# Eight-batch attention and spline FFN kernel: TensorE's loop turned elsewhere, the first batch's gathers in a row, and two kinds of products merged

## The reference

```python
h = depthwise_causal_conv(x, cond[:, None, :]) + cond_b          # 8 taps
q, k, v = split(h @ qkv_w.T + qkv_b)                             # 16 heads of 32
s = q @ k.T / sqrt(32) + slope[h] * (key - query)                # ALiBi, causal
x = x + softmax(where(causal, s, -1e9)) @ v @ out_w.T + out_b
Q, K, V = W @ x[b]          # c = the 256 rows, t = the 512 channels; 16 heads of 16
a = (Q.T @ K / 4 + b0) * m + (1 - m) * -1e30                     # m = cond[b], over keys
y = softmax(a) @ V
gate_w, up_w, down_w = catmull_rom(control_points)               # 2048 x 512 each
x = x + (silu(y @ gate_w.T) * (y @ up_w.T)) @ down_w.T
```

## Time and profile before

| | us |
|---|---|
| median of 3 runs | 1441.94 |
| lowest, highest | 1441.18, 1443.64 |
| the profiled execution, its own time | 1434.63 |
| its span, first to last instruction | 1432.8 |
| busy: TensorE, its weight loads | 1244.2, 725.6 |
| busy: VectorE, ScalarE, GpSimd | 755.2, 521.8, 359.6 |

### The profile page before, as it was taken

One profiled execution on the slowest core, in us unless ns is written; L12 is line 12 of the kernel. 1 busy time (PEld: TensorE's weight loads), 2 busy tenths in 40 slices (PEclk: granted clock), 3 DMA queues, 4 the chain that ended last, 5 costly groups with the idle time before them and its releaser, 6 DMA issues.

```text
span 1432.8 us, 23277 instructions
## 1 busy us (share of the span) xinstructions
PE 1244.2 (87%) x8680; PEld 725.6 (51%) x8680; DVE 755.2 (53%) x1173; ACT 521.8 (36%) x698; POOL 359.6 (25%) x203
## 2 busy tenths in 40 slices
PE   4485379899889999899999999899998998999988
PEld 3152135555455555556455555555455564656445
DVE  5354463547534673457724575346733577346732
ACT  1221145323532245223542245223552235423562
POOL 3079810055000830038000650009200380000000
PEclk9697579999989999999998999799998999999999
DMA  9857722366043731256042650337222560437124
GB/s 330 236 197 204 220 83 59 98 159 185 6 105 120 175 106 46 61 164 215 22 104 82 145 173 15 91 124 193 84 54 53 165 214 22 104 124 189 62 104 162
DMA packets 80495, 181.12 MB, mean 126 GB/s; under 512 B 14404, under 2 KB 54292, under 8 KB 70708
## 3 DMA queue, kind: packets, MB, share of 16 engines
q1 hardware_dynamic: 78352, 175.21, 41.9%
q0 software_dynamic: 1280, 4.20, 1.1%
q10 hardware_dynamic: 768, 0.26, 0.1%
HBM read 106.41 MB, written 21.14 MB: 89 GB/s over the span
## 4 chain that ended last, share of the span: by engine, by line
PE 66%; DVE 12%; issue 5%; POOL 5%; SPq 5%; DMA 4%; ACT 2%; DVEq 0%; ACTq 0%; POOLq 0%
PE psum L1054 8%; PE psum L848 8%; PE psum L1004 7%; PE psum L890 6%; DVE max L760 5%; PE psum L891 4%; PE psum L892 4%; PE psum L854 4%; SPq L374 3%; PE psum L879 3%; PE psum L868 3%; PE psum L916 3%; PE psum L1040 3%; PE psum L973 2%; PE psum L938 2%
## 5 line engine op out<-in xcount | busy, mean ns | idle before, releaser
L760 DVE TENSOR_REDUCE max<-psum 128x1 f32<-128x512 f32 x512 | 329.0, 685 | 113.0 <-PE psum L1004 110.9
L619 ACT ACTIVATE probs<-psum 128x1024 f32<-128x1024 f32 x256 | 248.8, 1022 | 119.0 <-PE psum L1040 118.3
L1004 PE MATMUL psum<-k,q 52*128 52x512 f32 x512 | 169.9, 514 | 75.4 <-DVE max L760 49.8
L505 POOL TENSOR_TENSOR h<-h_in,tap 128x1024 f32<-128x1024 f32 x7 | 13.3, 1900 | 701.3 <-DVE low L674 701.3
L1004 PEld LDWEIGHTS psum<-k,q 52*128 52x128 f32 x512 | 65.2, 191 | 197.8 <-DVE max L760 136.3
L580 ACT ACTIVATE probs<-psum 128x1024 f32<-128x1024 f32 x64 | 62.1, 1022 | 211.8 <-PE psum L959 211.8
L1054 PE MATMUL psum<-probs,v 128*32 128x256 f32 x2048 | 138.7, 389 | 0.4 <-ACT probs L619 0.3
L848 PE MATMUL psum<-h,qkv_w 128*128 128x256 f32 x512 | 119.8, 389 | 18.0 <-DVE h L653 18.0
L515 POOL TENSOR_TENSOR h<-h,products 128x1024 f32<-128x1024 f32 x49 | 128.0, 2611 | 3.8
L848 PEld LDWEIGHTS psum<-h,qkv_w 128*128 128x128 f32 x512 | 96.4, 193 | 39.1 <-issue 26.6
L890 PE MATMUL psum<-stack 128*128 128x512 f32 x256 | 113.7, 444 | 1.3 <-DVE stack L693 1.2
(11 more groups left out here) (106 smaller groups left out, 1722.9 us busy)
## 6 DMA issues: line engine op xcount, KB each, us to landing
stack<-wd_sorted SPq DMA_DIRECT2D x64, 1024.0 KB, 5.8
stack<-high SPq DMA_DIRECT2D x128, 128.0 KB, 2.4
stack<-low SPq DMA_DIRECT2D x64, 128.0 KB, 2.4
q<-high SPq DMA_DIRECT2D x128, 64.0 KB, 3.4
k<-high SPq DMA_DIRECT2D x128, 64.0 KB, 2.3
wd_sorted<-stack SPq DMA_DIRECT2D x8, 1024.0 KB, 4.5
h_in<-in_x_lanes SPq DMA_DIRECT2D x9, 512.0 KB, 4.7
x<-in_x_rows SPq DMA_DIRECT2D x8, 512.0 KB, 5.8
```

Of the source, the lines that this page charges most:

```text
L619: nc.scalar.activation(probs[:, u // 2 % 2, u % 2 * 2:u % 2 * 2 + 2, :], psum[:, 2 + u % 2 * 2:4 + u % 2 * 2, :], ACT.Exp)\
L760: nc.vector.reduce_max(max2[:, g, e, i, t:t + 1], psum[:, s % 2, :], AX_X).then_inc(S["s2_max"], 1)
L1004: nc.tensor.matmul(psum[:, e, :], r(q2[rows, g, i, t * P:(t + 1) * P]), r(k2[rows, g, i, :]), start=True, stop=True).then_inc(S["s2_ready" ...
```

## The change

- **TensorE's loop.** The first scores with their transpose and `values(1)` leave the front of `batch` and become `scores1(b)`. It is called once ahead of `batch(0)` and at the end of each batch for the next one. The order of all products stays; the place at which `Fori` jumps back is another.
- The first scores' banks are swapped, so that only their second pair of heads waits for `v1_out`.
- **Gathers.** The ring has four slots in the first batch (`SORT`), GpSimd issues all eight pairs ahead of the convolution, SP stores one block ahead of each half of a stack group, and VectorE subtracts four blocks ahead of the window and the others behind its steps 1 to 4.
- **Values.** `values2(kt)` takes all 512 queries in one product of 512 columns.
- **Mask.** One bf16 product per head writes the two diagonal blocks of 128 x 128 (the block of later keys is no longer written: the maxima read only columns up to the diagonal block).
- VectorE splits the next batch's queries and keys (`split1`) ahead of `outputs`.

```diff
@@ SP, first batch
+                def store_sorted(n):
+                    sp.wait_ge(down_low, n + 1)
+                    sp.dma_start(wd_dram[n], stack1[:, n % SORT]).then_inc(sorted_stored[n % SORT], 16)
+
                 def stacks2(g):
                     for off, stack, blocks in ((0, q2, QUERY_BLOCKS), (1024, k2, KEY_BLOCKS)):
+                        if first:
+                            store_sorted(2 * g + off // 1024)
...
-                    if first:
-                        for n in (2 * g, 2 * g + 1):
-                            sp.wait_ge(down_low, n + 1)
-                            sp.dma_start(wd_dram[n], stack1[:, n % RING]).then_inc(sorted_stored[n % RING], 16)
-                    else:
+                    if not first:
@@ GpSimd
-                    for n in range(RING):
+                    for n in range(NT):
                         gather(n)
...
-                    if first and k > TAPS - 1 - (NT - RING):
-                        gather(k)
@@ VectorE
+                for n in range(SORT if first else 0):
+                    sort(n)
                 for n in range(NT + 1):
-                    if first and n < NT:
-                        dve.wait_ge(down_high, n + 1)
...
+                    if first and 0 < n <= NT - SORT:
+                        sort(SORT - 1 + n)
@@ TensorE
-            def batch(b, first=False, last_batch=False):
+            def scores1(b):
...
-                    nc.tensor.matmul(bank[:, 0:L], ident_b[:], mask_q[:], start=False, stop=False,
-                                     skip_group_check=True)
-                    last = nc.tensor.matmul(bank[:, L + P:2 * L], ident_b[:], mask_q[:, 0:P], start=False, stop=True,
+                    last = nc.tensor.matmul(bank.rearrange("p (a n) -> p a n", n=P)[:, 0:LT * LT:3, :], ident_b[:],
+                                            mask_q[:, None, :].broadcast_to([P, 2, P]), start=False, stop=True,
                                             skip_group_check=True)
...
+                values(1)
+
+            def batch(b, first=False, last_batch=False):
...
-                        last = nc.tensor.matmul(psum[e * BLK:(e + 1) * BLK, 6, queries], v2[:, kt, head, :],
-                                                probs[:, kt % 2, e, queries], start=kt + half == 0, stop=kt == CT - 1,
+                        last = nc.tensor.matmul(psum[e * BLK:(e + 1) * BLK, 6, :], v2[:, t, head, :],
+                                                probs[:, t % 2, e, :], start=t == 0, stop=t == CT - 1,
                                                 skip_group_check=True)
...
                 turn_outputs(NG - 1)
+                if not last_batch:
+                    scores1(b + 1)
```

72 lines of the change are left out of this document (37 added, 35 removed).

## The result

The changed kernel takes 1416.68 us (median of 4 runs, 1416.06 to 1423.35), the kernel before 1441.56 (4 runs on the same chip, 1436.23 to 1443.64): a ratio of 0.984, interval 0.980 to 0.988. It is faster, by 25 us or 1.6%. The forecast was 1387 us, a gain of 51 us on the profiled execution's scale. That execution took 1434.63 us before and takes 1416.06 us now, 18.6 us less. The range (1376 to 1402) does not hold the result.

The account below looks back on a forecast made before the run. TensorE's own sequence and waits were taken as the bound. Turn 29.7, mask 4.2, values 0.6 and first batch 16.5 gave 51.0 us: 1434.6 to 1383.6, set at 1387 us between clock and offset readings; range 1376 to 1402.

Parts of the forecast that it names:

- The turn: TensorE's loop jump between batches: moved behind value products, its idle time and low clock go at five turns, 29.7 us.
- I leave 0.1 us uncovered per turn, and no fall of the clock: At TensorE's five jumps: value products hide nearly all the wait and the clock stays up; 0.5 us deducted from 30.2.
- the turn is half covered: Rival at TensorE's jump: a later or longer fetch leaves 1.5 us per turn, clock kept; 1394 us, chance 0.12.
- 108 ns: The skill's compare-and-branch cost: the jump term would be 0.5 us, not 29.7, and the kernel 1421 us; chance 0.03.
- The mask: First scores: one mask product per head in place of two saves 0.6 us per batch in batches 1 to 7, 4.2 us.
- the floor of VectorE: First scores: VectorE's maxima, 1.97 us after 0.31 us of waiting, let through only 0.2 to 0.3 us per two pairs.
- The values: Value products of 512 queries: eight instructions in place of sixteen save 5 ns per round over 128 rounds, 0.6 us.
- The first batch: Batch 0: gathers issued ahead of the convolution bring the first shifted product from 189.43 to 173, a gain of 16.5 us.
- 48 stack DMAs at 2.50 / 4 = 0.63 us: SP's queue in batch 0: issuing the stacks makes 30.0 us of 39.6 us in all, first shifted product at 170.3.
- The floor of the DMA engines, 173: Batch 0: 53 us of DMA work from 116 and some 4 us lost put the first shifted product at about 173.
- SP is held by its own stores: Rival in batch 0: stacks wait for sorted blocks, so the first batch gains only 5 us; 1398.5 us, chance 0.17.
- the offset of 7.3 us: Whole kernel: the runs' median lay 7.3 us above the profiled execution; clock at the turns (1384) or plain offset (1391).

Follow-up runs that it names:

- e8_mask_only: The kernel before with one mask product per head alone, and 16 instructions of padding ahead of batch 0: 1426.13 us, ratio 0.990.
- e4_turn_only: The kernel before with only TensorE's loop turned and the first scores' banks swapped: 1407.3 us, ratio 0.979.
- e3_pad32: The changed kernel with 16 tiny products, 32 instructions, added ahead of TensorE's loop: 1401.93 us, ratio 0.976 to the kernel before.
- e9: The changed kernel with 32 instructions of padding and stores of sorted blocks 4 to 7 moved behind the first max rows: 1398.48 us, ratio 0.976.
- e14: As e9, but the one mask product per head has all 512 columns in place of 256: 1385.54 us, ratio 0.966.
- e12_values_only: The kernel before with the values of all 512 queries in one product alone: 1441.84 us in one execution.
- e7_small_stores: The changed kernel with each sorted block's store cut to 1 partition of 128, whole blocks stored behind the max rows: 1421.13 us in one execution.
- e10: As e9, but two mask products per head (256 and 128 columns), and the loop's top 48 instructions further on: 1389.68 us, ratio 0.968.
- e15: The changed kernel with late stores, two mask products and 128 instructions of padding, the loop's top 176 instructions on: 1406.93 us, ratio 0.979.

## Why the prediction was wrong

**The turn (29.7 us forecast).** The reading of the earlier trace rows held: the 3.95 us were the jump's, TensorE's sequencer comes to it while the value products still run, and idle time and low clock at the five turns are down by 29.9 us, some 2.5 us of it the shorter mask pass (0.5 us per batch in e8_mask_only). e4_turn_only is 30 us faster than before. What failed is the sentence "I leave 0.1 us uncovered per turn, and no fall of the clock". It took the jump's measured length for the whole cost, wherever the code lies. The second fetch behind the jump left 2.3 to 2.6 us per turn uncovered (12.0 us, or 8.2 net of the low clock that stood there before). Low clock behind it cost 3.4. Fetches that fell on SP's stacks cost 5.5, and the low clock at the head of three windows, where before one had it, most of another 3.9. That this last clock follows from the longer wait ahead of it is read from the stages and not shown by a run. e3_pad32 gets some 15 of these 21 us back. The rival that the turn is half covered was this case: it said a fetch that starts later, and priced it at 1.5 us per turn and with the clock kept, too low on both. The Trainium skill's 108 ns (Advanced Engine Details and Errata, Control Flow Timing), weighed in the prediction, is out for a jump that is taken: it lasts 3.3 to 3.6 us here. The branch that falls through takes 0.08.

**The mask (4.2 us).** No gain from this step is to be seen in the turned kernel. 0.12 us per head and the floor of VectorE were read rightly, and 0.5 us per batch at full clock is there (e8_mask_only, 12 us faster in all). The step failed in asking only for TensorE's time, when the earlier trace rows show VectorE 1.97 us busy for each 0.31 us of waiting. A shorter product there makes TensorE wait, and the clock fell in those waits: with 256 columns 13 us more than with 512 (e9 and e14), and with one product 4 to 9 us more than with two, by medians of kernels that also differ in place. That the clock might fall for that was in no rival.

**The values (0.6 us).** Right in size: nothing that can be measured. The shortest eight rounds of e12_values_only take 34.19 us for 34.21 before, some 3 ns per round for 5 forecast.

**The first batch (16.5 us).** 10.4 came. The working had "48 stack DMAs at 2.50 / 4 = 0.63 us". The mis-sized term is this one: the fours took 3.4 to 4.7 us behind each store, 29.3 us in all for 20.0. The rows of before had it: SP's fours right behind stores took 3.31 to 4.87 us there too, and I took the row of a four that stood behind none. e7_small_stores shows that the stores' bytes are the cause. The floor of the DMA engines, 173, was the better of the two sums, and they ran at 95% in the stretch. The rival "SP is held by its own stores" had the place and gave a gain of 5, too pessimistic. The late start of the window (10 us where I had 5) is of the same cause, and cost nothing by itself.

**The convolution, and the offset of 7.3 us.** The convolution stayed hidden, as read from the earlier trace rows: it ends at 189.1, before the 199 that was allowed, and is read at 213.4. The offset between profiled execution and median is 0.6 us in the changed kernel's runs.

The sum for the measured terms: 29.9 + 10.4 - 1.1 - 8.2 - 3.4 - 5.5 - 3.9 + 0.4 = 18.6 us.

A version that beats both is e14_one_of_512: the change, with late stores, 32 instructions of padding and one mask product of 512 columns. 1385.54 us, ratio 0.966 (0.961 to 0.970) where the change alone has 0.984 (0.980 to 0.988).

What stays open: how much of the 9 us between e10 and e9 is the mask and how much the place of the loop, why two products of 128 columns take 13 us more than one of 256, and why one product helped in the kernel before (12 us) and does not in the turned one.

## What to carry to other kernels

When code is moved around a loop's jump, ask where its top then lies in the 16 KB pieces of code, and try a few paddings: each is one line and moved this kernel by 15 us (changed kernel to e3) and 17 us (e10 to e15), which is more than most edits give. Count the instructions of an edit ahead of the loop too, with their weight loads and for every copy of the code, or two variants that seem to differ in one thing differ in two. Where TensorE waits for another engine in a dense stretch, a shorter product can save nothing and cost clock; time to spare there may be worth filling. And when a DMA's issue time is taken for a sum, take it from rows with the same DMAs ahead of it.

## What the runs showed that I had not expected

- A fetch of 16 KB of code right behind a jump holds TensorE's first product by 2.3 us or more, and the same code shifted by 32 instructions does not. Shifted by 256 it does again.
- Four stack DMAs on SP take longer when a fetch of code falls among them: 4.06 to 4.67 us in 25 of 25 stages, against 3.61 to 4.00 in 55 without one.
- The granted clock falls without a jump or a long idle stretch ahead: in first scores with waits of 1.75 us for VectorE it was 0.86, with waits of 1.37 us 1.00. Columns that change nothing in what is read of the scores took the kernel from 1398 to 1386 us, with the loop at the same place.
- A store of 1 MB makes the next four DMAs of 64 KB on the same queue take 3.4 to 4.7 us to issue instead of 2.4.
